# Mixture-of-experts decoder layer: the three expert weights in one array, and one table load per turn of the block loop in place of two

## The reference

```python
x = _layernorm(x + _L0_attn_ref(x), axis=-1)           # dilated attention, 16 heads of 16
x = _layernorm(x + _L0_xattn_ref(x, ctx_512, L0_xattn_Wq, L0_xattn_Wkv_expand, L0_xattn_Wout), axis=-1)
x = _layernorm(x + _L0_ffn_ref(x, L0_ffn_gate_w, L0_ffn_w_gate, L0_ffn_w_up, L0_ffn_w_down), axis=-1)
```

```python
probs = jax.nn.softmax(x @ gate_w, axis=-1)
w, sel = jax.lax.top_k(probs, K)
w = w / jnp.sum(w, axis=-1, keepdims=True)
...
g = jnp.einsum('ech,ehi->eci', xg, w_gate)
u = jnp.einsum('ech,ehi->eci', xg, w_up)
y = jnp.einsum('eci,eih->ech', jax.nn.silu(g) * u, w_down).reshape(E * C, H)
out = jnp.zeros((T + 1, H), x.dtype).at[t_slot].add(w_slot[:, None] * y)
```

## Time and profile before

| | before |
|---|---|
| median of 3 runs | 681.29 us (678.33 to 681.30) |
| the profiled execution | 684.91 us, span 683.1 us |
| busy share of the span: PE, DVE, ACT, POOL | 79%, 56%, 53%, 51% |
| mean granted TensorE clock | 0.934 |
| turns of the block loop, blocks | 19, 152 |

### The profile page before, as it was taken

One profiled execution on the slowest core, in us unless ns is written; L12 is line 12 of the kernel. 1 busy time (PEld: TensorE's weight loads), 2 busy tenths in 40 slices (PEclk: granted clock), 3 DMA queues, 4 the chain that ended last, 5 costly groups with the idle time before them and its releaser, 6 DMA issues.

```text
span 683.1 us, 18720 instructions
## 1 busy us (share of the span) xinstructions
PE 537.2 (79%) x5130; PEld 413.6 (61%) x5131; DVE 383.3 (56%) x1761; ACT 359.8 (53%) x1253; POOL 347.8 (51%) x541
## 2 busy tenths in 40 slices
PE   2788788888888888884039998998898989885994
PEld 2455455555555554542028887887788878884883
DVE  1457777777777777764114454544444544452773
ACT  2466676666666666762015665665565656560111
POOL 6352445455555545545406776676676767670000
PEclk9999999999999999995559999999999999997998
DMA  9999999222222111222864555555555555558981
GB/s 199 274 260 374 349 339 339 86 77 77 77 77 77 67 67 73 85 77 88 283 207 144 178 168 162 164 176 155 167 160 153 175 158 165 153 157 327 419 324 48
DMA packets 83457, 121.35 MB, mean 178 GB/s; under 512 B 13779, under 2 KB 73181, under 8 KB 81376
## 3 DMA queue, kind: packets, MB, share of 16 engines
q1 hardware_dynamic: 62880, 77.74, 37.6%
q0 software_dynamic: 13824, 37.78, 15.5%
q10 hardware_dynamic: 6720, 5.41, 2.6%
HBM read 56.07 MB, written 69.01 MB: 183 GB/s over the span
## 4 chain that ended last, share of the span: by engine, by line
PE 59%; DVE 14%; ACT 10%; issue 10%; DMA 3%; ACTq 2%; POOL 1%; SPq 0%; DVEq 0%; POOLq 0%
PE bank L721 15%; PE bank L738 10%; PE bank L711 6%; ACT pr L792 5%; PE bank L762 4%; PE bank L543 3%; PE bank L533 3%; PE bank L731 3%; PE bank L593 2%; PE bank L672 2%; PE bank L766 2%; DVE nmax L981 2%; ACTq L289 2%; PE bank L630 2%; ACT prT L798 2%
## 5 line engine op out<-in xcount | busy, mean ns | idle before, releaser
L502 POOL DMA_INDIRECT results<-ys,wcol x152 | 149.8, 986 | 26.0 <-POOL pscrap L491 21.2
L480 POOL DMA_INDIRECT queues<-x,xidx x128 | 126.1, 985 | 39.9 <-issue 39.9
L721 PE MATMUL bank<-wgu,xtT 128*128 x616 | 130.8, 337 | 0.1
L1165 DVE SCALAR_TENSOR_TENSOR tg<-th,bank 128x96 f32<-128x96 f32 x154 | 39.2, 254 | 119.3 <-ACT th L883 119.3
L711 PE MATMUL bank<-ident,xt 128*128 128x128 f32 x310 | 64.7, 291 | 52.3 <-issue 28.8
L721 PEld LDWEIGHTS bank<-wgu,xtT 128*128 128x128 f32 x616 | 100.8, 198 | 0.5 <-issue 0.4
L792 ACT ACTIVATE pr<-bank,nmax 128x128 f32<-128x128 f32 x256 | 90.7, 370 | 19.6 <-DVE nmax L981 19.2
L711 PEld LDWEIGHTS bank<-ident,xt 128*128 128x128 f32 x310 | 59.6, 199 | 68.1 <-issue 37.2
L890 ACT ACTIVATE ys<-bank,wcol 128x256 f32<-128x256 f32 x152 | 72.0, 474 | 46.0 <-PE bank L738 46.0
L738 PE MATMUL bank<-wd,hT 96*128 x304 | 93.4, 389 | 0.0
L875 ACT COPY xtT<-bank 128x256 f32<-128x256 f32 x155 | 56.6, 365 | 39.4 <-PE bank L711 36.7
(11 more groups left out here) (180 smaller groups left out, 934.6 us busy)
## 6 DMA issues: line engine op xcount, KB each, us to landing
xt<-queues SPq DMA_DIRECT2D x162, 160.0 KB, 2.2
results<-zeros SPq DMA_DIRECT2D x16, 1024.0 KB
wgu<-results SPq DMA_DIRECT2D x16, 1024.0 KB, 9.0
queues<-zeros SPq DMA_DIRECT2D x34, 160.0 KB, 5.5
wgu<-in_L_ffn_w_gate SPq DMA_DIRECT2D x4, 768.0 KB, 11.9
wgu<-in_L_ffn_w_up SPq DMA_DIRECT2D x4, 768.0 KB, 13.7
wd<-in_L_ffn_w_down SPq DMA_DIRECT2D x4, 768.0 KB, 13.5
queues<-zeros ACTq DMA_DIRECT2D x16, 160.0 KB
```

What stands on the lines that cost most here:

```text
L480: pool.indirect_dma_start(xg, bass.IndirectOffsetOnAxis(ap=xidx[:, par, k:k + 1], axis=0), x2[:, par, :], None, bounds_check=last_row, oob ...
L502: pool.indirect_dma_start(yr, bass.IndirectOffsetOnAxis(ap=wcol[:, u, 1:2], axis=0), ys[:, u, :], None, bounds_check=last_y, oob_is_err=Fa ...
L721: ins = pe.matmul(bank[2 + u % 2][:, 0:2 * INTER].rearrange("p (g i) -> p g i", g=2), xtT[:, u % 2, kk, :], wgu[:, bass.ds(e, 4 * INTER)]. ...
```

## The change

The three weights lie in one array `wall`, 640 numbers per expert and partition: 192 of gate, 192 of up, 256 of down (the last on 96 partitions alone). So one table number, expert times 640, serves both projections, the down projection adding a constant 384. `tab_d` and the DVE instruction that fills it go away. PE loads ten entries per turn from `tab_g`, starting at entry 6 of the turn: the first eight are the turn's own blocks (down), the last eight those two ahead (gate and up). Before the loop it loads two entries where it loaded eight. `wall` is as large as `wgu` and `wd` together, and the last stage cuts all of it into buffers: `YB` goes from 6 to 10.

```diff
-YB = 6
+YB = 10
+GU = 2 * 2 * INTER
+WX = GU + D
...
-        wgu = sb("wgu", [P, NE * 2 * 2 * INTER])
-        wd = sb("wd", [INTER, NE * D])
+        wall = sb("wall", [P, NE * WX])
...
-            return wgu[:, k * YW:(k + 1) * YW]
+            return wall[:, k * YW:(k + 1) * YW]
...
-                sp.dma_start(wgu_v[:, e:e + 8, 0, :], gate_v[:, e:e + 8, :]).then_inc(experts_loaded, 16)
-                sp.dma_start(wgu_v[:, e:e + 8, 1, :], up_v[:, e:e + 8, :]).then_inc(experts_loaded, 16)
-                sp.dma_start(wd[:, e * D:(e + 8) * D].rearrange("i (e d) -> i e d", d=D),
-                             down_v[:, e:e + 8, :]).then_inc(experts_loaded, 16)
+                sp.dma_start(wall_v[:, e:e + 8, 0:GU // 2], gate_v[:, e:e + 8, :]).then_inc(experts_loaded, 16)
+                sp.dma_start(wall_v[:, e:e + 8, GU // 2:GU], up_v[:, e:e + 8, :]).then_inc(experts_loaded, 16)
+                sp.dma_start(wall_v[0:INTER, e:e + 8, GU:WX], down_v[:, e:e + 8, :]).then_inc(experts_loaded, 16)
...
-                pe.matmul(bank[6 + u % 2][:, 0:D], hT[:, u % 2, :], wd[:, bass.ds(e, D)],
+                pe.matmul(bank[6 + u % 2][:, 0:D], hT[:, u % 2, :], wall[0:INTER, bass.ds(e, WX)][:, GU:WX],
                           start=True, stop=True).then_inc(peF["y"], 1)
...
-            for t, e in zip((0, 1), neighbours(ET.PE, tab_g[0:1, 0:UN], (NE - 1) * 4 * INTER)[LEAD:]):
+            for t, e in zip((0, 1), neighbours(ET.PE, tab_g[0:1, LEAD:UN], (NE - 1) * WX)):
                 gu(t, t, e)
             turn_h(0, 0)
             with pe.Fori(0, rounds) as j:
-                e_gu = neighbours(ET.PE, tab_g[0:1, bass.ds(j * UN + UN, UN)], (NE - 1) * 4 * INTER)
-                e_down = neighbours(ET.PE, tab_d[0:1, bass.ds(j * UN, UN)], (NE - 1) * D)
+                e = neighbours(ET.PE, tab_g[0:1, bass.ds(j * UN + LEAD, UN + 2)], (NE - 1) * WX)
                 for u in range(UN):
                     t = j * UN + u
                     block_T(t + 3, u + 3, j)
-                    gu(t + 2, u, e_gu[u])
+                    gu(t + 2, u, e[u + 2])
                     turn_h(t + 1, u + 1)
-                    down(t, u, e_down[u])
+                    down(t, u, e[u])
...
-                for tab, first, times, plus in ((tab_g, LEAD, 4 * INTER, 0), (tab_w, LEAD, 1, D), (tab_d, 0, D, 0)):
+                for tab, first, times, plus in ((tab_g, LEAD, WX, 0), (tab_w, LEAD, 1, D)):
```

More of the change, by code:

```diff
@@ L190, in build @@
         tab_x = sb("tab_x", [1, TAB + 2 * LEAD], I32)
-        tab_d = sb("tab_d", [1, TAB], I32)
         tab_p = sb("tab_p", [1, NE], I32)
@@ L232, in build @@
         peH = Steps(sem("peH"), "count place table")
-        dveH = Steps(sem("dveH"), "took nblk nblkb skipb cum past tp n n2 fe fx tg tw td tx")
+        dveH = Steps(sem("dveH"), "took nblk nblkb skipb cum past tp n n2 fe fx tg tw tx")
         peF = {n: sem(f"peF_{n}") for n in ("xT", "gu", "hT", "y")}
@@ L255, in build @@
         down_v = w_down.rearrange("e i d -> i e d")
-        wgu_v = wgu[:, :].rearrange("p (e g k) -> p e g k", e=NE, g=2)
+        wall_v = wall[:, :].rearrange("p (e w) -> p e w", e=NE)
         block = stack.enter_context(nc.Block())
@@ L722, in gu @@
                                     xtT[:, u % 2, kk, :],
-                                    wgu[:, bass.ds(e, 4 * INTER)].rearrange(
+                                    wall[:, bass.ds(e, GU)].rearrange(
                                         "p (g k i) -> p g k i", g=2, k=2)[:, :, kk, :],
```

## The result

| | before | changed |
|---|---|---|
| median | 680.56 us (678.33 to 681.30) | 718.58 us (718.37 to 718.76) |
| ratio, 95% interval | | 1.056 (1.054 to 1.059) |
| the profiled execution | 684.91 us, span 683.1 | 718.37 us, span 716.6 |
| mean granted TensorE clock | 0.934 | 0.919 |

The account below looks back on a forecast made before the run. PE's pauses at the block loop's turn starts, filled by two table loads, were taken as the bound. For the median: 681.3 - 15.2 (second load) + 0.5 (ten numbers) - 3.0 (clock) = 663.6 us, range 659 to 670.

Parts of the forecast that it names:

- The bound: Block loop: PE's pauses ahead of each turn, 19 of 1.32 to 1.84 us, lie on the path, filled by table loads.
- The second load goes: PE's turn start: dropping the `tab_d` load and its register instruction saves 0.75 us, 0.98 at four pauses, 15.2 in all.
- The first load carries ten numbers instead of eight: PE's `tab_g` load at each turn's start: two more numbers cost 0.5 us over the loop, range 0 to 2.8.
- The rival that the load falls into pieces: PE's load from entry 6: two fetches of 593 ns give 678 us, three 689.5; chance 0.05, of which slower 0.02.
- The rival of a load paid by the number: PE's `tab_g` load: two more numbers cost 2.8 us and the clock drops stay, 668.9 us; chance 0.07.
- The clock: Block loop: three slow-clock turns vanish with shorter pauses, 4.5 us less, 3.0 counted for the median.
- Never behind a shorter one: Block loop: the three slow-clock turns each follow a pause above 1.7 us, never one of the fifteen shorter.
- The offset of 384: Down projection: one more register operation, 0.014 us in each of 152 blocks, hidden by PE's array; 0, uncovered 2.1 us.
- The fill of `tab_d`, the stride of the weights: Ahead of the loop: one DVE instruction less and weight DMAs writing with another stride, both hidden by waits; nothing.
- Ten buffers instead of six: Last stage: reading further ahead gives no gain and doesn't delay output DMAs; 0.
- the rival of that name: Last stage, output behind reads: DMAs served in issue order make output late, about 6 us more, 669.6; chance 0.06.
- POOL as the pace: Rival in the loop: POOL holds each turn up 0.2 us, giving 3.8 us back, 667.4; chance 0.02.

Follow-up runs that it names:

- The kernel with kept registers: Changed kernel, but PE loads eight numbers per turn from a multiple of eight and keeps the last two for the next turn; ratios 0.981, 0.983, 0.985, 0.982.

## Why the prediction was wrong, step by step

- *The bound* was read rightly: the pauses at a turn's start are the loads and lie on the path. All of the change's effect went through them.
- *The second load goes*, 15.2 us: it went, and the fused register instruction with it. Alone it can't be seen in the result. The kernel with kept registers, which has one short load per turn as the forecast wanted, has pauses of 0.77 us at its turns' starts, against 28.8 / 19 = 1.52 before. That is 0.75 less, the forecast's figure, though from another chip and a kernel with other pauses besides.
- **The first load carries ten numbers instead of eight: this step failed.** I took 0.5 us for the loop, with 2.8 as the upper end. It was (2618 - 708) ns x 19 = 36.3 us, 35.8 more than counted. For the profiled execution the sum was 665.7, and 718.4 was measured: of these 52.7 us the load has 35.8 and the clock 13.9 (+9.4 instead of -4.5); 2.0 more of pauses and the 1.0 of start and last stage are left. I had compared the duration of one number on PE with that of eight on DVE, both amid the traffic ahead of the loop, and read from it that the content hardly counts. That pair hid what counts: eight from an aligned start are two fetches, one number is one, and the rest was most likely the traffic (one number took 962 ns there, 308 at the quiet end). No row had a start inside a group of four, so the bound of 2.8 was a bound on the wrong variable. The 7.6 us that the Trainium skill's figure (Runtime: NRT & Kernel Launch, section Instruction fetch mechanics) gave were too low as well, since they costed only the two added numbers and not the eight that lost their fetches of four.
- *The rival that the load falls into pieces* had the mechanism: an unaligned start, and a turn to slower from 1.35 us per load on. It had 5%, of which 2% slower, and its pieces were too few and too dear: three of 0.59 us against ten of 0.24. It named "one per number" as well, without pricing it. The rival of a load paid by the number had the count of pieces but a price of 0.074 us each (593 ns over eight), a third of the 0.23 that a start off a multiple of four costs.
- *The clock.* That kernels with longer pauses have more slow turns held, in both directions: none in the loop with pauses up to 1.35 us (ten numbers from a multiple of eight, 1.00), eight with 2.5 to 3.1. Turn by turn it does not hold: ten of the changed kernel's turns behind pauses of 2.60 to 2.97 us were granted 1.00, while one behind 2.50 was slow, and before, the longest pause of all, 1.84, had no slow turn behind it. What picks the turn is open. "Never behind a shorter one" also left out the loop's first turn, slow behind a pause of 1.38 us (its granted clock was 0.85). The forecast -4.5 became +9.4 in the profiled pair. That kernel with ten aligned numbers shows the sizes: idle time down by 32.0 - 25.9 = 6.1 us, busy time by 229.5 - 223.2 = 6.2, its profiled execution 672.01 us, 12.9 less than 684.91. Between medians it is 6.9, little more than the idle time. That suggests that the median execution of the kernel before has little of the clock's loss in it, and that of the 3.0 that I counted for it most was not there to gain; no trace of such an execution was kept.
- *The offset of 384*, counted as nothing: held. In the kernel with ten aligned numbers, which has the offset too, PE's timeline has

```profile
382.08 0.50 PE L710 MATMUL bank<-ident,xt 128*128 128x128 f32 x2 [1.24 <-issue]
...
394.97 0.50 PE L710 MATMUL bank<-ident,xt 128*128 128x128 f32 x2 [1.16 <-issue]
```

  a turn of 12.89 us with a pause of 1.16, so 11.73 of work; before, 13.19 less 1.47 was 11.72.
- *The fill of `tab_d`, the stride of the weights*, nothing: held. The loop begins at 356.6 instead of 356.1.
- *Ten buffers instead of six*, nothing: held. ACT's first output DMA to its last takes 46.1 us against 46.2, with reads that land after 19.0 us instead of 9.0, and the output DMAs themselves land after a median of 4.6 us against 4.5. Output does not wait behind the reads, and the rival of that name falls.
- *POOL as the pace*: never tested at 680 us; where a mid-turn pause came in, it was DVE's.

## What to carry to other kernels

When a register load is given another start or count, count its fetches before its numbers: round the start down and the count up to multiples of four entries of 4 bytes (counted from the table's first entry), even if some of what is read is thrown away. A price read from loads of one form says nothing of another form, so where the profile has no row for the new form, its bound is the worst way in which it could be carried out, number by number, and not the size of the added part. And a longer pause on TensorE is to be counted with the clock behind it.

## What the runs showed of the hardware

- A register load of one number takes 0.31 us at a quiet time, each further fetch 0.23 to 0.26, and a fetch is four numbers where the load starts at a multiple of four entries, else one (eight numbers: 0.59 us from entry 4, 1.93 from entry 1, 2 or 6). Twelve numbers (0.85 us) are faster than ten (1.08), four (0.33) than two (0.54). DVE shows the same (ten from entry 6: 2.29 us).
- A load of four ahead of a matmul was hidden where the array was still busy (0.05 us between matmuls) and left a pause of 0.47 us right behind a wait for DVE.
- Useless work can buy back clock that idle time costs: three useless matmuls (2.76 us) under each 2.6 us load raised the granted clock of the loop from 0.88 to 1.00 and made the kernel 3% faster (864.5 to 837.1 us).
- The time of one kernel, the one before, was 680 us in the first measurements and 815 to 820 us, a fifth more, on four other chips later, without a cause that was found.
